# A head's mean square as two float32r products of parts that lie in the outputs' place, with VectorE's order by chunk changed

## The reference, cut to what matters

```python
Sf, o = jax.lax.scan(step, S0, (qh, kh, vh, gh))
mu = jnp.mean(o, axis=-1, keepdims=True)
var = jnp.var(o, axis=-1, keepdims=True)
o = (o - mu) * jax.lax.rsqrt(var + 1e-05)
o = jax.nn.silu(g) * o
x = x + o @ Wo
```

## Time and profile before

| | |
|---|---|
| median of 3 runs | 1599.29 us (1598.97 to 1599.48) |
| the profiled execution | 1597.72 us, its span 1596.0 us |
| granted TensorE clock | 0.999 over the span |
| PE | 1576.8 us busy, 99% of the span, 12274 instructions |
| DVE | 847.4 us, 53% |
| ACT | 567.2 us, 36% |
| POOL | 162.5 us, 10% |

### The profile page before, as it was taken

The page is one execution under the profiler, slowest core; times in us unless marked ns, Lnnn a source line. Parts: engine busy times, 40 slices in busy tenths (PEclk is TensorE's granted clock), DMA queues, the critical chain, the costliest instruction groups (busy, mean ns, idle before and its releaser), DMA issues.

```text
span 1596.0 us, 30636 instructions
## 1 busy us (share of the span) xinstructions
PE 1576.8 (99%) x12274; PEld 1275.5 (80%) x12274; DVE 847.4 (53%) x1320; ACT 567.2 (36%) x988; POOL 162.5 (10%) x190
## 2 busy tenths in 40 slices
PE   7999999999999999999999999999999999999998
PEld 5888787787777777777777888888888888888887
DVE  5554555467797887978887451331415132241513
ACT  4333344276564655736555411111111111111111
POOL 1222331100221102201020100000000000000000
PEclk9999999999999999999999999999999999999999
DMA  7443442101020211202123423030300203030110
GB/s 160 142 101 92 119 112 73 60 28 42 22 87 3 87 43 47 87 3 87 61 82 123 142 96 136 0 138 0 138 0 30 108 0 138 0 138 0 63 44 27
DMA packets 50757, 114.08 MB, mean 71 GB/s; under 512 B 13322, under 2 KB 24666, under 8 KB 42467
## 3 DMA queue, kind: packets, MB, share of 16 engines
q1 hardware_dynamic: 47906, 99.95, 19.3%
q10 hardware_dynamic: 1152, 8.39, 1.3%
q0 software_dynamic: 1600, 4.25, 1.3%
HBM read 78.98 MB, written 33.59 MB: 71 GB/s over the span
## 4 chain that ended last, share of the span: by engine, by line
PE 90%; DVE 6%; ACT 1%; issue 1%; DMA 1%; SPq 1%; DVEq 0%; PEld 0%; ACTq 0%; PEldq 0%
PE m_ps L1569 9%; PE m_ps L1568 9%; PE m_ps L1567 9%; PE a_ps L161 7%; PE a_ps L163 7%; PE a_ps L162 7%; PE f_ps L161 6%; PE f_ps L163 5%; PE f_ps L162 5%; PE m_ps L1589 4%; PE m_ps L1590 4%; PE m_ps L1588 4%; PE a_att L1312 3%; PE a_ps L1431 2%; PE a_ps L1333 2%; DVE row L1843 1%
## 5 line engine op out<-in xcount | busy, mean ns | idle before, releaser
L1817 DVE TENSOR_TENSOR m_h<-m_ps,m_silu 128x512 f32<-128x512 f32 x85 | 58.7, 690 | 392.9 <-PE m_ps L1569 392.9
L1567 PE MATMUL m_ps<-m_xshi,m_w 128*128 128x512 f32 x680 | 266.2, 392 | 0.0
L1569 PE MATMUL m_ps<-m_xshi,m_w 128*128 128x512 f32 x680 | 264.7, 389 | 0.0
L1568 PE MATMUL m_ps<-m_xslo,m_w 128*128 128x512 f32 x680 | 264.6, 389 | 0.0
L1883 ACT ACTIVATE m_silu<-m_ps 128x512 f32<-128x512 f32 x85 | 50.7, 597 | 325.8 <-PE m_ps L1569 325.8
L1569 PEld LDWEIGHTS m_ps<-m_xshi,m_w 128*128 128x128 f32 x680 | 127.6, 188 | 26.6
L1567 PEld LDWEIGHTS m_ps<-m_xshi,m_w 128*128 128x128 f32 x680 | 127.7, 188 | 26.4 <-issue 0.2
L1568 PEld LDWEIGHTS m_ps<-m_xslo,m_w 128*128 128x128 f32 x680 | 127.7, 188 | 26.3 <-issue 0.2
L1045 DVE TENSOR_TENSOR a_a<-a_att,causal 128x1024 f32<-128x1024 f32 x64 | 75.2, 1216 | 11.8 <-PE a_att L1312 11.8
L1893 ACT ACTIVATE m_h0hi<-m_h 128x512 fp32r<-128x512 f32 x45 | 28.5, 633 | 132.0 <-DVE m_h L1817 132.0
L1588 PE MATMUL m_ps<-m_h0hi,m_w 128*128 128x512 f32 x188 | 73.1, 389 | 0.0
(11 more groups left out here) (318 smaller groups left out, 3484.5 us busy)
## 6 DMA issues: line engine op xcount, KB each, us to landing
row<-scratch_xn SPq DMA_DIRECT2D x16, 1024.0 KB, 4.8
row<-scratch_xmid SPq DMA_DIRECT2D x16, 1024.0 KB, 7.3
m_xt<-in_L_attn_W SPq DMA_DIRECT2D x33, 256.0 KB, 3.0
f_xt<-in_L_attn_x SPq DMA_DIRECT2D x32, 256.0 KB, 7.8
scratch_xn<-row SPq DMA_DIRECT2D x8, 1024.0 KB, 8.6
scratch_gate<-row ACTq DMA_DIRECT2D x8, 1024.0 KB, 3.9
scratch_xmid<-row SPq DMA_DIRECT2D x8, 1024.0 KB, 4.9
row<-scratch_gate SPq DMA_DIRECT2D x8, 1024.0 KB, 10.4
```

What stands on the lines that cost most here:

```text
L1567: pe.matmul(ps, wh, xh, start=k == 0, stop=False)
L1568: pe.matmul(ps, wh, xl, start=False, stop=False)
L1569: ins = pe.matmul(ps, wl, xh, start=False, stop=k == LAST)
L1817: dve.tensor_tensor(h[n], dense.region(f"b{j}"), silu[n], ALU.mult).then_inc(dense.taken_sem(f"b{j}"), 1)
```

## The change

`avg32` is filled so that it can be read as float32r. ScalarE's square still goes to `sq`; a copy of it rounded to float32r goes to `og_hl[0]` at the chunk's tokens, and VectorE writes the rest to `og_hl[1]` (`squares_lo`). TensorE multiplies both parts by `avg32`, in two float32r products into one bank. Since the outputs' own parts come to lie in the same place, `gated` is taken apart: `weigh_out` (the gate's silu times `oc`, in place in the row buffer), `over_deviation` (times `rn`, in place) and `gated_parts` (the two parts), and these stand at other places of VectorE's order. ScalarE's `deviation` moves ahead of the inverse deviation of chunk 2, and `rn` may be written again when `over_deviation` of the chunk before is done.

```diff
                     if c > 0:
                         dve.wait_ge(*mix.ready(c - 1, i))
+                        squares_lo(i, c - 1)
...
                     ahead(("c0", "u", "c2", "c3")[c])
+                    if c == 2:
+                        over_deviation(i, 0)
+                    if c == NC - 1:
+                        gated_parts(i, 0)
+                        over_deviation(i, 1)
+                        gated_parts(i, 1)
...
                     if c > 0:
-                        gated(i, c - 1)
+                        weigh_out(i, c - 1)
+                over_deviation(i, NC - 2)
+                gated_parts(i, NC - 2)
+                squares_lo(i, NC - 1)
+                weigh_out(i, NC - 1)
                 ahead("gates")
-                gated(i, NC - 1)
+                over_deviation(i, NC - 1)
+                gated_parts(i, NC - 1)
...
+            def squares_lo(i, c):
+                dve.wait_ge(*count.at("squares", i, 3 * c + 2))
+                dve.tensor_tensor(og_hl[1][:, :, tokens(c)], sq, og_hl[0][:, :, tokens(c)].bitcast(F32),
+                                  ALU.subtract).then_inc(count.sem("squares"), 1)
+            def weigh_out(i, c):
+                part = gsilu[:, :, tokens(c)]
+                dve.wait_ge(*dense.taken(f"g{LAST}", i))
+                dve.wait_ge(*mix.taken(c, i))
+                dve.tensor_tensor(part, part, oc, ALU.mult).then_inc(count.sem("og"), 1)
+            def over_deviation(i, c):
+                out = gsilu[:, :, tokens(c)]
                 dve.wait_ge(*count.at("rn", i, c + 1))
                 dve.wait_ge(*count.at("og", i, 2 * c + 1))
+                dve.tensor_tensor(out, out, rn, ALU.mult).then_inc(count.sem("og"), 1)
+            def gated_parts(i, c):
+                hi, lo = (part[:, :, tokens(c)] for part in og_hl)
+                out = gsilu[:, :, tokens(c)]
                 dve.wait_ge(*count.at("og", i, 2 * c + 2))
+                dve.tensor_copy(hi, out).then_inc(count.sem("oghi"), 1)
                 dve.wait_ge(*count.at("oghi", i, c + 1))
+                dve.tensor_tensor(lo, out, hi.bitcast(F32), ALU.subtract).then_inc(count.sem("oglo"), 1)
...
                     squares(i, ((0, 1), (2,), (3,), ())[c])
+                    if c == NC - 1:
+                        deviation(i)
                     if c > 0:
                         inverse_deviation(i, c - 1)
-                    if c == NC - 1:
-                        deviation(i)
                     act.wait_ge(*mix.ready(c, i))
                     ps = mix.region(c)
-                    act.activation(flat(sq), ps, ACT.Square).then_inc(count.sem("sq"), 1)
+                    act.activation(flat(sq), ps, ACT.Square).then_inc(count.sem("squares"), 1)
+                    act.wait_ge(*count.at("squares", i, 3 * c + 1))
+                    act.activation(og_hl[0][:, :, tokens(c)], sq, ACT.Copy).then_inc(count.sem("squares"), 1)
                     if c > 0:
                         act.wait_ge(*count.at("og", i, 2 * (c - 1) + 1))
...
                 if c > 0:
-                    act.wait_ge(*count.at("oglo", i, c))
+                    act.wait_ge(*count.at("og", i, 2 * c))
...
-                pe.wait_ge(*count.at("sq", i, c + 1))
+                pe.wait_ge(*count.at("squares", i, 3 * c + 3))
...
-                pe.matmul(ps, avg32, flat(sq), start=True, stop=True).then_inc(dense.ready_sem(f"var{c}"), 1)
+                pe.matmul(ps, avg32.bitcast(F32R), og_hl[0][:, :, tokens(c)], start=True, stop=False)
+                pe.matmul(ps, avg32.bitcast(F32R), og_hl[1][:, :, tokens(c)], start=False, stop=True).then_inc(dense.ready_sem(f"var{c}"), 1)
```

More of the change, by code:

```diff
@@ L210, in step, with select @@
         pool.wait_ge(s_fill, n)
-    def select(ap, op, base, pattern, cm, fill):
-        step(pool.affine_select(out=ap, in_=ap, compare_op=op, fill=fill, base=base,
+    def select(ap, op, base, pattern, cm, fill, dt=F32):
+        step(pool.affine_select(out=ap.bitcast(dt), in_=ap, compare_op=op, fill=fill, base=base,
                                 pattern=pattern, channel_multiplier=cm))
@@ L229, in fill_constants @@
     a = avg32.rearrange("p (a b) -> p a b", b=32)
-    select(a, ALU.is_ge, 0, [[-32, 4], [0, 32]], 1, 0.0)
-    select(a, ALU.is_ge, 31, [[32, 4], [0, 32]], -1, 0.0)
+    select(a, ALU.is_ge, 0, [[-32, 4], [0, 32]], 1, 0.0, F32R)
+    select(a, ALU.is_ge, 31, [[32, 4], [0, 32]], -1, 0.0, F32R)
     step(pool.memset(avg_all, 1.0 / D))
@@ L846, in phase_a @@
                           ("state", GR * (NC - 2)), ("first", NC - 1), ("weighing", NC),
-                          ("sq", NC), ("rn", NC), ("og", 2 * NC), ("oghi", NC), ("oglo", NC)):
+                          ("squares", 3 * NC), ("rn", NC), ("og", 2 * NC), ("oghi", NC), ("oglo", NC)):
             count.add(name, per)
@@ L1081, in body @@
                                                           ALU.add).then_inc(dense.taken_sem(f"o{m}"), 1)
-            def gated(i, c):
+            def squares_lo(i, c):
[9 more added lines that the diff above has]
+                out = gsilu[:, :, tokens(c)]
                 dve.wait_ge(*count.at("rn", i, c + 1))
-                dve.tensor_tensor(rn, rn, oc, ALU.mult).then_inc(count.sem("og"), 1)
-                dve.wait_ge(*dense.taken(f"g{LAST}", i))
                 dve.wait_ge(*count.at("og", i, 2 * c + 1))
-                dve.tensor_tensor(rn, rn, gsilu[:, :, tokens(c)], ALU.mult).then_inc(count.sem("og"), 1)
+                dve.tensor_tensor(out, out, rn, ALU.mult).then_inc(count.sem("og"), 1)
+            def gated_parts(i, c):
+                hi, lo = (part[:, :, tokens(c)] for part in og_hl)
+                out = gsilu[:, :, tokens(c)]
                 dve.wait_ge(*count.at("og", i, 2 * c + 2))
-                dve.tensor_copy(og_hl[0][:, :, tokens(c)], rn).then_inc(count.sem("oghi"), 1)
+                dve.tensor_copy(hi, out).then_inc(count.sem("oghi"), 1)
                 dve.wait_ge(*count.at("oghi", i, c + 1))
-                dve.tensor_tensor(og_hl[1][:, :, tokens(c)], rn,
-                                                og_hl[0][:, :, tokens(c)].bitcast(F32), ALU.subtract).then_inc(count.sem("oglo"), 1)
+                dve.tensor_tensor(lo, out, hi.bitcast(F32), ALU.subtract).then_inc(count.sem("oglo"), 1)
             def first_row(part):
```

## The result

| | before | after |
|---|---|---|
| median of 4 runs | 1599.24 us (1598.97 to 1599.48) | 1624.74 us (1619.61 to 1627.2) |
| ratio, 95% interval | | 1.0155 [1.0142, 1.0168] |
| profiled execution, its span | 1597.72, 1596.0 us | 1624.02, 1622.3 us |
| first body, next six, last body up to o0 | 66.9, 65.7, 38.6 us | 74.5, 68.1 to 68.2, 42.3 us |
| gates' first step (L963) after the body's start, bodies 1 to 6 | 31.6 us | 34.4 us |

The forecast was 1612.0 us with a range up to 1620: slower, as said, but by 25.5 us where 12.7 were forecast. Bodies are counted from 0, so that bodies 1 to 6 are the second to the seventh. A body's start is here the product that transposes `khat` of chunk 0 (L1396 before, L1424 after). The gap of the spans, 26.3 us, splits into 7.6 in the first body, 6 x 2.45 in the next six, 3.7 in the last and 0.3 ahead. Phase M takes the same time as before.

What follows compares the result with a forecast made beforehand. PE (99% busy) and VectorE's chain from the gates' first step to g3 bound a body at once. 7 x 1.5 + 2.2 = 12.7 us on 1597.72, plus 1.6 to the median, gave 1612.0 us, range 1604 to 1620.

Steps and rivals of the forecast that it cites:

- PE's gain: Mean square's product on TensorE: two float32r products save 0.38 us per chunk, 12.2 us over 32 chunks.
- The eleven steps: VectorE's steps between chunk 3's mask and the gates' first step, summed to 6.59 us.
- the gates' first step: VectorE's L963 in the second body: starts at 463.13 instead of 461.12, 2.0 us later (1.2 to 2.8).
- PE waited for L963 seven times: At chunk 3's mean square, PE waits some 1.8 us for z0's bank, once in each of seven bodies.
- the forecast wait of z1 on the Ln: PE at z1 waits some 0.9 us for ScalarE's Ln of chunk 2, seven times.
- g3 follows the offsets: PE's g3, already level with VectorE's chain: offsets start 1.6 us later and g3 with them; +1.5 us per body taken.
- `over_deviation` of chunk 0 ends at 450.05: VectorE step behind chunk 2's mask in the second body, priced at 0.69 us; ScalarE's Ln for chunk 1 waits for it.
- Seven bodies give 10.5 us: All bodies but the last, first included, lose 1.5 us each.
- a fall of the clock: PE's new waits close its clock gate: counted within the rival cases, with no chance or size of its own.
- The last body, +2.2 forecast: Last body, without gates' sums: first output product o0 starts at 864.8 instead of 862.4; net +2.2 us (1.5 to 3).
- `squares_lo` of chunk 3: VectorE in the last body: starts at 859.2, ends at 859.9, behind nine steps (5.37 us); PE's mean square needs it.
- one of 4: Last body: a PE wait of 4 us ahead of the mean square, on the squares' rest.

Runs made afterwards that it cites:

- e2: Changed kernel without the four VectorE subtractions `squares_lo`; TensorE multiplies the first part twice, so the mean square is twice too large; 1608.65 us.
- e1: Changed kernel with the new order alone: one float32 product of `sq` as before, no rounded copy, no subtraction of the squares; 1614.71 us.
- e5_slot33: Changed kernel with GpSimd's third sum moved off `over_deviation` of chunk 0 and TensorE's loop head at place 33 instead of 163; 1625.46 us.
- after_slot33: Changed kernel with the head of TensorE's loop code at place 33 instead of 163, nothing else; 1630.15 us.
- e5_sum_earlier: Changed kernel with ScalarE's square for GpSimd's third sum one chunk earlier, so the sum leaves `over_deviation` of chunk 0 alone; 1621.7 us.
- e6: Changed kernel with GpSimd's scaling of the next row's input held until VectorE's offsets are made; 1620.11 us.
- e12: Changed kernel with the rest of chunk 1's squares left out (8 of 512 columns subtracted, first part multiplied twice); 1620.18 us.
- e3: Changed kernel with the outputs' parts of chunks 0, 1 and 2 moved behind the gates' sums on VectorE; 1624.15 us.
- e14: e3 plus chunk 3's first product behind the gates, e5_sum_earlier's edit, GpSimd's scaling held until the weighings; 1606.67 us at loop place 33, 1620.81 at 163.
- e8: e3 with e6's edit added, GpSimd's scaling held until the offsets are made; 1622.21 us.
- e10: Kernel before with the mean square as two float32r products, but `gated` in one piece and the old order; 1629.2 us.

## Why the prediction was wrong

Right were the direction, the place and most sizes. The products are 0.23 us apart, and PE's gain is 0.39 us per chunk (e2 against e1; 0.38 in the prediction). The eleven steps took what was summed. With the disturbances away the gates' first step is 0.1 us from the forecast (e5_slot33). PE waited for L963 seven times, but 1.4 us, since the gap had already made PE late; for the same reason the forecast wait of z1 on the Ln did not show (without the gap both are there, 1.6 and 0.8 us in after_slot33). g3 follows the offsets as said: +2.8 us at the gates became +2.35 at g3.

The terms that failed, against 12.7 us:

- "`over_deviation` of chunk 0 ends at 450.05", priced at 0.69 us. It took 1.35 beside GpSimd's sum, and 0.68 in e2 and e5 where it ran alone. The gates came 0.8 us later than forecast and the bodies 0.9 longer: 5.6 us over bodies 1 to 6. Moving the sum alone gave back only 0.2 to 0.5 us at the gates (e5_sum_earlier), because the stop in the weights was next in line; with both away the gates came 0.7 us sooner and two undisturbed bodies took 67.4 us, where the forecast has 67.2. So of the 0.9 about 0.7 is the doubled step and 0.2 the forecast's own. I had worked out when VectorE's steps would start, but not laid GpSimd's beside them.
- "Seven bodies give 10.5 us" took the first body as like the others. It lost 7.6 us and not 1.5. Of the 6 us 4.2 are GpSimd's scaling on the scans and offsets (e6). For the rest, 1.8 us, chunk 2's mean square came late behind the stop in the weights, in a stretch at a granted clock of 0.50. Where the clock stayed at 1.00 behind the same stop the first body's gates stood at 34.6 to 34.7 us and not at 36.5 (e12, e5_sum_earlier, against the changed kernel and e6), which is 1.9 us; no run changed the clock alone. The prediction had left a fall of the clock to its rivals and given it no price.
- The last body, +2.2 forecast, +3.7 measured. It is the first term again. `squares_lo` of chunk 3 started 36.9 us after the body's start and the forecast has 35.4; the mean square waited for it and o0 came as far behind it as forecast. All of that is there at chunk 3's mask already, at 28.0 and not at 26.6; 1.1 us of it is the `over_deviation` of chunk 0, which took 1.77. Moving the sum alone did not give it back: in e5_sum_earlier the mask came at 26.9, but the two weight steps behind it then waited 0.8 us for ScalarE, behind products of PE with a stop of 1.2 us in them for which the profile names nothing, and o0 came at 42.1. The waits fell otherwise than forecast, 2.60 us at z1's bank and 0.64 ahead of the mean square in place of one of 4: z1's bank is released behind the Ln of chunk 2 (POOLq L146 in the list of waits), and the Ln waits for `over_deviation` of chunk 1. That wait, forecast for the other seven bodies, was left out for this one; it cost nothing by itself, since the mean square still had to wait for `squares_lo`.

These make 13.1 of the 13.6 us by which the spans' gap exceeds the forecast. In bodies 1 to 6 the stop in the weights is not among them: without it the changed kernel's gates stand where they stood, and its total is no better (after_slot33). It costs 8 us in e3 and 14 in e14, where VectorE no longer hides it.

Open stays what sets the time of the fetch. The code of e2 is the changed kernel's at the same places, its packet came 18.7 to 19.1 us into the body and not 21.2 to 21.5, and it had no gap; e1 and the kernel before, whose packets came at 18.5 to 19.0, had none either. Taking away the mask's wait (e12) brought the packet to 20.8, and the gap stayed.

## What to carry to other kernels

Before pricing a step that moves, lay every other engine's steps that read or write the same memory beside its new time, GpSimd's above all: a VectorE step of 0.7 us cost 1.35 to 1.8 there, and what started GpSimd's scaling here was a load that did not move with VectorE. A faster engine moves loads forward too, and the margin may be used up by that. When a loop on TensorE is near 2048 places of code, look whether its packets of code grow with the number of its bodies, and time one kernel at two places of the loop's head before a small difference is put down to arithmetic.

## What the hardware showed that I had not expected

- VectorE beside a GpSimd product or sum of 128 x 512: product 0.69 to 1.35 or 1.78 us, cast 0.43 to 1.40 or 1.52, subtraction 0.69 to 1.66, the pair of offsets 2.36 to 4.37, a scan group 1.37 to 2.42. The Trainium skill, SBUF — State Buffer, section SBUF: two separate sides, says that a VectorE operation with two inputs in SBUF and a GpSimd operation that reads it lock each other out for the whole instruction. The products, the subtractions and the offsets, all with two inputs, agree; that a cast with one input waits too the page has only for a faster mode, and no run here tells which mode it was in.
- The place of one loop's head changed the time by 17 us with identical instructions (1624.74 and 1641.31 us), and a loop whose places ended at 1960 was not fetched again in its bodies, while the same loop ending at 2090 was fetched whole in each.
- After the same gap of 1.5 us the granted clock fell in one body of e3 (0.72 over 6 us, products 0.43 us apart: the 1.2 GHz level) and not in others. Bodies 1 to 5 of one execution with and without that fall differ by 1.6 to 1.9 us (e3, e5_sum_earlier, e8, e10), and what decides which body it hits no run tells.
